# Three feed-forward streams written out with constant waits, their gates spread by DMA instead of by TensorE, and a clamp done by a Relu on ScalarE

## The chip, the cores and the metric

The kernel runs on one NeuronCore of a Trainium2 chip. The metric is device time in microseconds, taken as the median of repeated runs of the whole program. Before the change it is 1961.65 us (three runs, 1959.19 to 1965.57). The engines are named as in the profile: PE is TensorE, PEld its weight loads, DVE is VectorE, ACT ScalarE, POOL GpSimd, and SP issues most of the DMAs.

## The reference

The program is a model of four layers over 2048 tokens of 128 features. Each layer normalises `x`, computes an attention branch `s` and a feed-forward branch, and adds `s * silu(ffn)`:

```
for each layer:
    xn = layernorm(x)
    s  = attention(xn)
    g  = silu(ffn(xn))
    x  = x + s * g
```

The change touches the feed-forward branches of layers 1, 2 and 3, cut here to the core.

```
# layer 1: ternary weights, 512 hidden units (4 blocks of 128)
h   = relu(x @ Wq1.T + b1)
out = h @ Wq2.T + b2

# layer 2: 16 experts of 64 hidden units, 4 chosen per token, and a shared pair
g, u   = silu(x @ w1_e.T), x @ w3_e.T
routed = einsum('tef,ehf,te->th', g * u, w2_e, combine)      # combine: gate of token t for expert e
out    = routed + shared

# layer 3: 16 experts of 128 hidden units, 4 chosen per token
gate = minimum(x @ Wgate_e + bg, 7.0)
up   = clip(x @ Wup_e + bu, -7.0, 7.0)
act  = (up + 1) * gate * sigmoid(1.702 * gate)
out  = einsum('te,teh->th', scores, act @ down_e + down_bias)
```

All experts are computed for all tokens; the gates of the experts that a token did not choose are zero.

## The kernel before

Activations are kept transposed, features on the 128 partitions and tokens along the free axis (`xnT`, 128 x 2048), and worked on in four chunks of 512 tokens (`CHUNK`, `NCH` = 4). A feed-forward branch is a *stream* of steps. One step takes one block of 128 hidden units for one chunk: one or two "up" products of 128 x 512 into PSUM (`f_a`, `f_b`), the activation and the products with the gate on ScalarE and VectorE (`f_act`, `f_mid`, `f_hid`), and one "down" product that accumulates into `f_y`. After the last block of a chunk, ScalarE applies Silu to `f_y` and writes the layer's gate `gT`. The stages are called f1 (layer 1: 4 blocks per chunk, 16 steps), f2 (layer 2: 8 blocks that each hold two routed experts, and one shared block, 36 steps) and f3 (layer 3: 16 experts, 64 steps).

The class `Stream` (L721 to L853) serves all three. It writes one chunk (f1 and f3) or a chunk's steps inside a hardware loop (`Fori`), with waits on register values. There are two PSUM tiles each of `f_a`, `f_b` and `f_g`, and one `f_y`. PE issues the up products of the next step ahead of the down product of the current one.

A token's gate is one number per expert and token, and it has to stand on all 128 partitions to be multiplied into the hidden units. Before, TensorE does that: the gates are split into three bf16 parts (`split3`, L551), the parts are turned by TensorE (`turn_parts`, L1177) and kept as `r_gateT` (48 x 2048 bf16). In each routed step one bf16 product with a 0/1 matrix (`f_g<-r_gateT,r_r_pick`, L769) adds the three parts up and spreads the gate over the partitions, in PSUM, where VectorE's `f_hid` (L850) reads it.

In f3, VectorE clamps: `f_gated` (L822) adds the bias to `f_a` and takes the minimum with 7, then ScalarE computes Silu with slope 1.702 (`f_act`, L801); VectorE computes `f_linear` (L832) from `f_b`, `f_mid` (L836) and `f_hid` (L850). The down bias enters as a product with f32 gates, `f_y<-r_r_gateT,l_down_bias` (L780), first in each chunk.

The routers (`GroupRouter` for layer 2, `SoftmaxRouter` for layer 3, L1146 to L1336) compute the gates during the attention stage of the same layer (a2a, a3a). Their products on TensorE are jobs that a planner in `causal_attention` sets between the attention's own ones, by costs that each router states (`PE_NS`, `DVE_NS`, `CHAIN_NS`).

Of the kernel before, what the change touches and what calls it, by code (L numbers as in the profile page):

```python
# [718 lines left out]


class Stream:  # L721

    def __init__(self, nc, k, ph, J, func, up, down, gate=None, hidden_bias=None, out_bias=0.0, first=None, clamp=None):
        self.nc, self.k, self.J, self.func, self.up, self.down = nc, k, J, func, up, down
        self.gate = gate or (lambda j: None)
        self.hidden_bias, self.out_bias, self.first, self.clamp = hidden_bias, out_bias, first, clamp
        self.U = 1 if J % 2 == 0 else 2
        self.a = [ph.ps(f"a{i}") for i in range(2)]
        self.b = [ph.ps(f"b{i}") for i in range(2)] if len(up(0)) == 2 else None
        self.g = [ph.ps(f"g{i}") for i in range(2)] if gate else None  # L740
        self.y = ph.ps("y")
        self.hid = ph.sb("hid", [P, 2, CHUNK])
        if self.b:
            self.act, self.mid = ph.sb("act", [P, 2, CHUNK]), ph.sb("mid", [P, 2, CHUNK])
        if clamp:
            self.gated, self.linear = ph.sb("gated", [P, 2, CHUNK]), ph.sb("linear", [P, 2, CHUNK])
            self.gated_ready, self.linear_ready = ph.sem("gated"), ph.sem("linear")
        self.up_done, self.act_ready, self.mid_ready = ph.sem("up_done"), ph.sem("act_ready"), ph.sem("mid_ready")
        self.hid_ready, self.hid_used, self.y_read = ph.sem("hid_ready"), ph.sem("hid_used"), ph.sem("y_read")
        self.per = self.U * J  # L750

    def steps(self):

        return [(u, j, u * self.J + j) for u in range(self.U) for j in range(self.J)]

    def chunk(self, tensor, i, u):
        return tensor[:, bass.ds((i * self.U + u) * CHUNK, CHUNK)]

    def tensor(self, pe):
        nc, J, per = self.nc, self.J, self.per  # L760
        pe.sem_inc(self.hid_used, 2)
        with pe.Fori(0, NCH // self.U) as i:
            def up(u, j, n):
                pe.wait_ge(self.hid_ready, i * per + n + 1)
                x = self.chunk(self.k.xnT, i, u)
                for bank, weight in zip((self.a, self.b), self.up(j)):
                    mm = nc.tensor.matmul(bank[n % 2][:], weight, x, start=True, stop=True)
# [2 lines left out]
                mm.then_inc(self.up_done, 1)  # L770

            steps = self.steps()
            up(*steps[0])
            for (u, j, n), after in zip(steps, steps[1:] + [None]):
                if after:
                    up(*after)
                if j == 0:
                    pe.wait_ge(self.y_read, i * self.U + u + 1)
                    if self.first:
                        nc.tensor.matmul(self.y[:], self.first[0], self.chunk(self.first[1], i, u), start=True, stop=False)  # L780
                pe.wait_ge(self.hid_ready, i * per + n + 3)
                nc.tensor.matmul(self.y[:], self.down(j), self.hid[:, n % 2, :], start=(j == 0 and not self.first),
                                 stop=(j == J - 1)).then_inc(self.hid_used, 1)

    def scalar(self, act, between=None):

        act.sem_inc(self.y_read, 1)
        if not self.b:
            act.sem_inc(self.hid_ready, 2)
        if between:  # L790
            self.scalar_chunks(act, 0, 1)
            between()
        self.scalar_chunks(act, 1 if between else 0, NCH // self.U)

    def scalar_chunks(self, act, begin, end):
        nc, J, per = self.nc, self.J, self.per
        with act.Fori(begin, end) as i:
            for u, j, n in self.steps():
                if self.clamp:
                    act.wait_ge(self.gated_ready, i * per + n + 1)  # L800
                    nc.scalar.activation(self.act[:, n % 2, :], self.gated[:, n % 2, :], self.func,  # L801
                                         scale=self.clamp["slope"]).then_inc(self.act_ready, 1)
                elif self.b:
                    act.wait_ge(self.up_done, i * per + n + 1)
                    nc.scalar.activation(self.act[:, n % 2, :], self.a[n % 2][:], self.func).then_inc(self.act_ready, 1)
                else:
                    act.wait_ge(self.up_done, i * per + n + 1)
                    act.wait_ge(self.hid_used, i * per + n + 1)
                    nc.scalar.activation(self.hid[:, n % 2, :], self.a[n % 2][:], self.func,
                                         bias=self.hidden_bias[:, j:j + 1]).then_inc(self.hid_ready, 1)  # L810
                if j == J - 1:
                    act.wait_ge(self.hid_used, i * per + n + 3)
                    nc.scalar.activation(self.chunk(self.k.gT, i, u), self.y[:], ACT.Silu,
                                         bias=self.out_bias).then_inc(self.y_read, 1)

    def vector(self, dve):
        nc, per = self.nc, self.per
        dve.sem_inc(self.hid_ready, 2)
        with dve.Fori(0, NCH // self.U) as i:
            def gated(n, j):  # L820
                dve.wait_ge(self.up_done, i * per + n + 1)
                nc.vector.tensor_scalar(self.gated[:, n % 2, :], self.a[n % 2][:], self.clamp["gate_bias"][:, j:j + 1],  # L822
                                        self.clamp["limit"], ALU.add, ALU.min).then_inc(self.gated_ready, 1)

            for u, j, n in self.steps():
                cur = n % 2
                if self.clamp:
                    gated(n, j)


                    limit = self.clamp["limit"]
                    nc.vector.tensor_scalar(self.linear[:, cur, :], self.b[cur][:], self.clamp["up_bias"][:, j:j + 1],  # L832
                                            limit + 1.0, ALU.add, ALU.min).then_inc(self.linear_ready, 1)
                    dve.wait_ge(self.linear_ready, i * per + n + 1)
                    dve.wait_ge(self.act_ready, i * per + n + 1)
                    nc.vector.scalar_tensor_tensor(out=self.mid[:, cur, :], in0=self.linear[:, cur, :], scalar=1.0 - limit,  # L836
                                                   in1=self.act[:, cur, :], op0=ALU.max, op1=ALU.mult).then_inc(self.mid_ready, 1)
                else:
                    dve.wait_ge(self.act_ready, i * per + n + 1)
                    if self.gate(j) is None:  # L840
                        dve.wait_ge(self.hid_used, i * per + n + 1)
                    out = self.hid if self.gate(j) is None else self.mid
                    mm = nc.vector.tensor_tensor(out[:, cur, :], self.b[cur][:], self.act[:, cur, :], ALU.mult)
                    mm.then_inc(self.mid_ready, 1)
                dve.wait_ge(self.mid_ready, i * per + n + 1)
                if self.gate(j) is None:
                    dve.sem_inc(self.hid_ready, 1)
                else:
                    dve.wait_ge(self.hid_used, i * per + n + 1)
                    nc.vector.scalar_tensor_tensor(out=self.hid[:, cur, :], in0=self.mid[:, cur, :],  # L850
                                                   scalar=1.0 / self.clamp["slope"] if self.clamp else 1.0, in1=self.g[cur][:],
                                                   op0=ALU.mult, op1=ALU.mult).then_inc(self.hid_ready, 1)
# [2323 lines left out]
```

## Time and profile before

| | us |
|---|---|
| Median of three runs | 1961.65 |
| Profiled execution, first to last instruction | 1961.1 |
| TensorE busy | 1627.6 (83%) |
| VectorE busy | 1264.4 (64%) |
| ScalarE busy | 890.3 (45%) |
| f1: first matmul to end of last gate activation | 44.09 |
| f2: the same | 113.50 |
| f3: the same | 216.01 |

The program is a sequence of stages with barriers between them, so that a stage's time is that of its own slowest chain. The three streams are 373.6 us of the span; the rest is attention and layer 0. The granted TensorE clock, averaged over the span, is 0.886 of full speed. In the row of the page that gives it by slice its forty digits run from 5 to 9 tenths (9 stands for 0.9 or more).

### The profile page before, as it was taken

How to read it: one execution, taken by the hardware profiler on the slowest of the kernel's cores; microseconds unless marked ns; L12 is line 12 of the kernel's file. 1: busy time of each engine (PE TensorE's matmuls, PEld its weight loads, DVE VectorE, ACT ScalarE, POOL GpSimd, SP SyncE). 2: the span in 40 equal slices, each digit the busy share in tenths (PEclk: the TensorE clock that was granted, in tenths of full speed). 3: DMA queues.
4: the chain of work that ended last, by engine and by line, in shares of the span. 5: the costliest groups of instructions: out<-in, count | busy, mean ns of one | idle time of the engine just before them, and what ended most of it. 6: DMA issues, size and time to landing. Idle time of an engine off the chain costs nothing. (4 is left out here: it accounts for less than half of the span.)

```text
span 1961.1 us, 33261 instructions
## 1 busy us (share of the span) xinstructions
PE 1627.6 (83%) x12241; PEld 758.7 (39%) x12241; DVE 1264.4 (64%) x2588; ACT 890.3 (45%) x1711; POOL 481.8 (25%) x417
## 2 busy tenths in 40 slices
PE   6989737988888888887579888899659889899998
PEld 4665413433333333343224334333323434343333
DVE  4334768586586676734678888244668887358887
ACT  2332234666565665664236665422316666432221
POOL 1603266565566566410300000000200100000000
PEclk7998856989998998997779999699759999599999
DMA  7232277566575576501421100000340100000000
GB/s 208 89 81 73 62 202 196 154 171 158 148 185 150 149 183 156 132 1 27 138 45 35 34 19 2 1 1 0 90 129 18 35 19 19 1 0 1 0 0 21
DMA packets 211407, 153.63 MB, mean 78 GB/s; under 512 B 57600, under 2 KB 192184, under 8 KB 211128
## 3 DMA queue, kind: packets, MB, share of 16 engines
q1 hardware_dynamic: 201000, 134.90, 26.5%
q10 hardware_dynamic: 8208, 12.52, 2.2%
q0 software_dynamic: 2048, 4.20, 0.7%
q8 instruction: 94, 1.54, 0.3%
q14 instruction: 57, 0.47, 0.1%
HBM read 83.48 MB, written 67.37 MB: 77 GB/s over the span
## 5 line engine op out<-in xcount | busy, mean ns | idle before, releaser
L1936 DVE TENSOR_REDUCE a1a_partial<-a1a_room 128x4 f32<-128x1024 f32 x192 | 225.7, 1220 | 28.3 <-PE a1a_room L2001 27.7
L2376 ACT ACTIVATE a3a_probsT<-a3a_st 128x512 f32<-128x512 f32 (+2 forms) x320 | 155.7, 560 | 131.0 <-PE a3a_st L2442 79.2
L1895 ACT ACTIVATE a1a_probsT<-a1a_st 128x512 f32<-128x512 f32 (+1 forms) x416 | 205.1, 574 | 18.3 <-PE a1a_st L2034 17.5
L2376 ACT ACTIVATE a2a_probsT<-a2a_st 128x512 f32<-128x512 f32 (+2 forms) x320 | 155.6, 560 | 125.3 <-PE a2a_st L2442 73.3
L2288 DVE TENSOR_REDUCE a3a_maxima<-a3a_room 128x2 f32<-128x1024 f32 (+3 forms) x160 | 170.2, 1112 | 38.7 <-PE a3a_room L2411 24.8
L2288 DVE TENSOR_REDUCE a2a_maxima<-a2a_room 128x2 f32<-128x1024 f32 (+3 forms) x160 | 170.2, 1112 | 28.8 <-PE a2a_room L2411 19.1
L2071 PE MATMUL a1a_ctx<-a1a_probsT,a1a_vpad 128*9 128x512 f32 (+3 forms) x1408 | 148.4, 520 | 1.5
L1800 POOL TENSOR_TENSOR a1a_shifted<-a1a_shifted,a1a_best 128x1024 f32<-128x1024 f32 x64 | 121.8, 1903 | 101.8 <-DVE a1a_best L1942 101.7
L1932 DVE CUSTOM_DVE_ANT_0 a1a_shifted<-a1a_room,a1a_bands 128x256 f32<-128x256 f32 x256 | 93.3, 421 | 81.9 <-PE a1a_room L2001 77.1
L2001 PE MATMUL a1a_room<-stack 48*128 48x128 bf16 (+1 forms) x1376 | 110.9, 271 | 40.4 <-DVE a1a_partial L1936 20.7
L1898 ACT ACTIVATE a1a_probsT<-a1a_st 128x512 f32<-128x512 f32 x128 | 73.8, 602 | 129.7 <-PE a1a_st L2043 129.5
L2034 PE MATMUL a1a_st<-stack 51*128 51x512 bf16 (+3 forms) x576 | 113.2, 322 | 14.3 <-ACT a1a_nearT L1902 5.6
L801 ACT ACTIVATE f_act<-f_gated 128x512 f32<-128x512 f32 x64 | 40.3, 629 | 155.6 <-DVE f_gated L822 155.6
L2337 POOL COPY a_vpad<-a_values 128x256 f32<-128x256 f32 x16 | 6.3, 402 | 425.5 <-PE a3a_ctx L2454 209.8
L2435 PE MATMUL a3a_st<-stack 51*128 51x512 bf16 (+3 forms) x384 | 88.9, 357 | 18.5 <-DMA stack<-a3a_parts 9.5
L2435 PE MATMUL a2a_st<-stack 51*128 51x512 bf16 (+3 forms) x384 | 88.1, 354 | 15.5 <-ACT a2a_probsT L2376 8.0
L2454 PE MATMUL a3a_ctx<-a3a_probsT,a_vpad 128*32 128x512 f32 (+3 forms) x768 | 91.0, 552 | 7.7 <-ACT a3a_probsT L2376 4.7
L2001 PEld LDWEIGHTS a1a_room<-stack 48*128 48x128 bf16 x1376 | 47.7, 102 | 126.0 <-DVE a1a_partial L1936 57.8
L2454 PE MATMUL a2a_ctx<-a2a_probsT,a_vpad 128*32 128x512 f32 (+3 forms) x768 | 90.6, 550 | 4.2 <-ACT a2a_ctxT L2383 2.0
L1812 POOL TENSOR_TENSOR a1a_beyond<-a1a_probsT,c_beyond_mask 128x512 f32<-128x512 f32 x56 | 71.1, 1271 | 84.4 <-ACT a1a_probsT L1898 84.4
L2404 PE MATMUL a3a_room<-stack 48*128 48x512 bf16 (+3 forms) x384 | 68.5, 358 | 23.9 <-DMA stack<-k 14.1
L2404 PE MATMUL a2a_room<-stack 48*128 48x512 bf16 (+3 forms) x384 | 66.9, 350 | 25.5 <-PEq L2524 15.9
(500 smaller groups left out, 3276.6 us busy)
## 6 DMA issues: line engine op xcount, KB each, us to landing
a1a_bands<-a_band SPq DMA_DIRECT2D x112, 192.0 KB, 3.9
a_near<-a1a_shifted SPq DMA_DIRECT2D x112, 192.0 KB, 2.9
a1a_near<-a_near SPq DMA_DIRECT2D x64, 256.0 KB, 3.8
a_band<-a1a_r_mix SPq DMA_DIRECT2D x64, 254.0 KB, 3.5
stack<-q SPq DMA_DIRECT2D x96, 96.0 KB
stack<-k SPq DMA_DIRECT2D x32, 96.0 KB
l_inputs<-l_zeros SPq DMA_DIRECT2D x1, 2624.0 KB, 11.1
q<-a1j_parts ACTq DMA_DIRECT2D x10, 256.0 KB, 3.0
```

The source lines that it names most:

```text
L1800: nc.gpsimd.tensor_tensor(shifted[:, V % 2, t], shifted[:, V % 2, t], best[:, V % 2, :, t:t + 1].broadcast_to([P, HG, NEAR]), ALU.subtract ...
L1895: nc.scalar.activation(dst, src, ACT.Exp).then_inc(exp_done, 1)
L1932: ins = nc.vector.tensor_tensor_reduce(shifted[:, V % 2, t, place, :], src[:, place // 2, place % 2, :], band[i][:, place, :], 1.0, LOWEST ...
L1936: nc.vector.tensor_reduce(partial[:, g % 2, :, 1 + r].rearrange("p (a s) -> p a s", a=2), src, X_AXIS, ALU.max).then_inc(job_free, 1)
L2001: mm = nc.tensor.matmul(dst[:, lo + i * P:lo + (i + count) * P], q, rows_of(sides[edge], place, STACK)[:, c * P:(c + count) * P], start=Tr ...
L2034: mm = nc.tensor.matmul(dst[:, to:to + count * P], rows_of(sides[edge], place + j, ALL_ROWS)[:, c * P:(c + 1) * P], query_rows(q_stack, pl ...
L2071: mm = nc.tensor.matmul(ctx[32 * h:32 * h + DH + 1, lo * P:hi * P], vpad[b][right][:, c, h, :], probsT[:, block_index(V, at) % BLOCK_ROOMS ...
L2288: nc.vector.tensor_reduce(best, scores, X_AXIS, ALU.max).then_inc(job_free, 1)
L2376: nc.scalar.activation(probsT[:, block_at % BLOCK_ROOMS, place:place + heads, lo:], src, ACT.Exp).then_inc(exp_done, 1)
L2404: mm = nc.tensor.matmul(dst[:, end - width:end], query_rows(q_stack, place, STACK, I // HALF_TILES)[:, I % HALF_TILES * P:(I % HALF_TILES ...
L2435: mm = nc.tensor.matmul(dst[:, j * width:(j + 1) * width], rows_of(k_stack, place + j, ALL_ROWS)[:, c * P:(c + 1) * P], query_rows(q_stack ...
L2454: mm = nc.tensor.matmul(ctx[32 * PAIRED[h]:32 * PAIRED[h] + 32, lo:], vpad[b][:, c, PAIRED[h], :], probsT[:, block_at % BLOCK_ROOMS, h, lo ...
```

## The change

`Stream`, `run_stream`, `split3`, `turn_parts` and `split_gates` go, and each of the three streams is written out by hand.

- The steps are unrolled, and every wait is on a constant. `f_a` and `f_b` have three PSUM tiles each and `f_y` has two in f2 and f3; f1 has three `f_a` and one `f_y`. PE is two steps ahead with the up products (`AHEAD`). The Silu on `f_y` of a chunk is issued after one or two steps of the next chunk.
- The gates stay f32. They are turned once (`turn_gates`), kept as `r_gateT` (16 x 2048) and stored to DRAM (`store`, by SP, at the end of the attention block). During the stream SP loads them back, spread over 128 partitions, one 128 x 512 f32 tile (256 KB) for each routed step, into four tiles (`GateRows`, `KEPT`). The load for step m waits until the row of step m-4 has been used. VectorE waits for the landing ahead of `f_hid`. The product `f_g` is gone.
- In f3 the clamp moves to ScalarE: `below` = Relu(7 - gate - bias), then Silu(1.702 x 7 - 1.702 x below). VectorE keeps `f_linear`, `f_mid` and `f_hid`.
- The routers have fewer jobs (layer 3: three in place of five) and other costs for the planner. One constant, its load and GpSimd's two `pick` matrices go.

The diff, cut to its core (waits on tiles that are free again and the router's bookkeeping left out):

```diff
-def split3(nc, chain, src, parts, rest):
...
-class Stream:
...
-                if self.gate(j) is not None:
-                    mm = nc.tensor.matmul(self.g[n % 2][:], self.gate(j), self.chunk(self.k.gateT, i, u), start=True, stop=True)
...
+    def store(self, sp, job_free, count):
+        sp.wait_ge(job_free, count)
+        sp.dma_start(self.dram, self.gateT[:]).then_inc(self.stored, 16)
+        sp.wait_ge(self.stored, 16)
+
+class GateRows:
+    KEPT = 4
+    def load(self, sp, m, src, hid_ready, read_by):
+        if m >= self.KEPT:
+            sp.wait_ge(hid_ready, read_by)
+        sp.dma_start(self.of(m), src).then_inc(self.landed[m % self.KEPT], 16)
+    def wait(self, dve, m):
+        dve.wait_ge(self.landed[m % self.KEPT], 16 * (m // self.KEPT + 1))
...
 def grouped_ffn(nc, k, w, tiles, r):
+                for m in range(NCH * M):
+                    c, j = divmod(m, M)
+                    c0, j0 = divmod(m - rows.KEPT, M)
+                    src = over(r.dram[2 * j:2 * j + 2, c * CHUNK:(c + 1) * CHUNK], 1, P // 2)
+                    rows.load(sp, m, src, hid_ready, c0 * J + j0 + 1)
...
+                    rows.wait(dve, c * M + j)
+                    if n >= 3:
+                        dve.wait_ge(hid_used, n - 2)
+                    nc.vector.tensor_tensor(hid[:, n % 3, :], mid[:, n % 2, :], rows.of(c * M + j), ALU.mult).then_inc(hid_ready, 1)
...
 def clamped_ffn(nc, k, w, tiles, r):
+                for n in range(N):
+                    c, j = divmod(n, E)
+                    src = r.dram[j:j + 1, c * CHUNK:(c + 1) * CHUNK].broadcast_to([P, CHUNK])
+                    rows.load(sp, n, src, hid_ready, n - rows.KEPT + 1)
...
+                    nc.scalar.activation(below[:, n % 2, :], a[n % 3][:], ACT.Relu, bias=r.gate_room[:, j:j + 1], scale=-1.0).then_inc(below_ready, 1)
...
+                room_below(0)
+                for n in range(N):
+                    c, j = divmod(n, E)
+                    if n + 1 < N:
+                        room_below(n + 1)
+                    act.wait_ge(below_ready, n + 1)
+                    nc.scalar.activation(acted[:, n % 3, :], below[:, n % 2, :], ACT.Silu, bias=r.top[:, 0:1], scale=-SLOPE).then_inc(act_ready, 1)
+                    if c and j == AHEAD:
+                        gates_of(c - 1)
...
+                router.store(sp, job_free, jobs.index(("router", 0, router.JOBS - 1)) + 1)
```

`over(x, 1, 64)` repeats each row of `x` 64 times, so the source in f2 is 2 rows x 64 repeats x 512 numbers; in f3 it is one row repeated 128 times.

TensorE in f3, before: the first rows of the stage, and the loop that follows (`r_r_each` are the up weights, `l_w_down` the down weights).

```order
L767 MATMUL f_a<-xnT,r_r_each 128x512
L767 MATMUL f_b<-xnT,r_r_each 128x512
L769 MATMUL f_g<-r_gateT,r_r_pick 128x512
L778 REGISTER_ALU
L780 REGISTER_ALU
L780 MATMUL f_y<-r_r_gateT,l_down_bias 128x512
L781 REGISTER_ALU
L782 MATMUL f_y<-f_hid,l_w_down 128x512
L767 MATMUL f_a<-xnT,r_r_each 128x512
L767 MATMUL f_b<-xnT,r_r_each 128x512
L769 MATMUL f_g<-r_gateT,r_r_pick 128x512
```

TensorE in f3, of the changed kernel: the start of the stage.

```order
L1373 MATMUL f_a<-xnT,r_r_each 128x512
L1376 MATMUL f_b<-xnT,r_r_each 128x512
L1387 MATMUL f_y<-r_r_gateT,l_down_bias 128x512
L1389 MATMUL f_y<-f_hid,l_w_down 128x512
L1373 MATMUL f_a<-xnT,r_r_each 128x512
L1376 MATMUL f_b<-xnT,r_r_each 128x512
L1389 MATMUL f_y<-f_hid,l_w_down 128x512
```

`f_g` is gone, the register instructions too, and three steps' up products (of which the last is shown) stand ahead of the first `f_y`.

SP of the changed kernel, from the end of layer 2's attention to the next stage, with the shapes that the destination is written in.

```order
L2400 DMA stack<-a2a_parts 3x8x128 x6
L1059 DMA l_gates<-r_r_gateT 16x2048
L2318 UNCONDITIONAL_BRANCH
L1251 UNCONDITIONAL_BRANCH
L1079 DMA f_rows<-l_gates 128x1x512 x32
L1249 UNCONDITIONAL_BRANCH
```

The same of layer 3:

```order
L2400 DMA stack<-a3a_parts 3x8x128 x6
L1059 DMA l_gates<-r_r_gateT 16x2048
L2318 UNCONDITIONAL_BRANCH
L1359 UNCONDITIONAL_BRANCH
L1079 DMA f_rows<-l_gates 128x512 x64
L1357 UNCONDITIONAL_BRANCH
```

SP had no work in f2 and f3 before; now one store closes the attention block and 32 or 64 row loads stand in the stream.

ScalarE in f1, of the changed kernel (`l_b` holds the biases, `f_std` belongs to layer 1's attention output norm):

```order
L960 ACTIVATE f_hid<-f_a,l_b 128x512 x6
L953 ACT_TABLE_LOAD
L953 ACTIVATE gT<-f_y,l_b 128x512
L960 ACTIVATE f_hid<-f_a,l_b 128x512 x4
L953 ACTIVATE gT<-f_y,l_b 128x512
L949 ACT_TABLE_LOAD
L949 ACTIVATE f_std<-f_std 128x16
L960 ACTIVATE f_hid<-f_a,l_b 128x512 x4
L953 ACT_TABLE_LOAD
L953 ACTIVATE gT<-f_y,l_b 128x512
L960 ACTIVATE f_hid<-f_a,l_b 128x512 x2
L953 ACTIVATE gT<-f_y,l_b 128x512
```

Each chunk of the loop before had one load ahead of its Relus and one ahead of its gate.

## Rows read from the trace of the kernel before

**Rows 1.** Busy time by stretch: columns, f1, f2, f3, then 884 to 896

```profile
core 0: us, PE busy (x) PEld busy (x) DVE busy (x) ACT busy (x) POOL busy (x), PEclk, DMA share, GB/s
872.56:916.65 44.09, 34.13 (x64) 13.07 (x64) 18.60 (x60) 24.91 (x30) 0.00 (x0) 0.88 0.00 0
1270.96:1384.46 113.50, 110.16 (x248) 41.10 (x248) 46.85 (x68) 25.91 (x42) 0.00 (x0) 1.00 0.00 0
1735.21:1951.22 216.01, 207.41 (x456) 75.29 (x456) 178.02 (x256) 47.48 (x72) 0.00 (x0) 0.98 0.00 0
884.00:896.00 12.00, 10.29 (x16) 3.96 (x16) 7.81 (x15) 5.16 (x8) 0.00 (x0) 0.72 0.00 0
```

**Rows 2.** In order of time, a step of f3: start us, us, engine, line

```profile
1746.90 1.12 PE L782 MATMUL f_y<-f_hid,l_w_down 128*128 128x512 f32 x2
...
1747.79 0.63 ACT L801 ACTIVATE f_act<-f_gated 128x512 f32<-128x512 f32 x1 [2.46 <-DVE f_gated L822]
...
1748.52 0.69 DVE L836 SCALAR_TENSOR_TENSOR f_mid<-f_linear,f_act 128x512 f32<-128x512 f32 x1
...
1749.25 0.69 DVE L850 SCALAR_TENSOR_TENSOR f_hid<-f_mid,f_g 128x512 f32<-128x512 f32 x1
...
1749.99 1.12 PE L782 MATMUL f_y<-f_hid,l_w_down 128*128 128x512 f32 x2
```

**Rows 3.** In order of time, f2's shared step, first and last of four

```profile
1294.93 1.02 PE L767 MATMUL f_a<-xnT,r_r_turned 128*128 x2
...
1297.51 1.02 PE L767 MATMUL f_a<-xnT,r_r_turned 128*128 x2
```

**Rows 4.** Groups by line: count, busy us, mean ns, idle before

```profile
L832 DVE TENSOR_SCALAR f_linear<-f_b,r_r_up_bias 128x512 f32<-128x512 f32 x64 | 47.4, 740 | 0.0
...
L769 PE MATMUL f_g<-r_gateT,r_r_pick 48*128 x96 | 37.3, 389 | 0.0
```

**Rows 5.** In order of time, a chunk's end in f3

```profile
1787.10 1.12 PE L782 MATMUL f_y<-f_hid,l_w_down 128*128 128x512 f32 x2 [1.97 <-DVE f_hid L850]
...
1788.36 0.60 ACT L813 ACTIVATE gT<-f_y 128x512 f32 x1 [2.83 <-PE f_y L782]
...
1788.97 1.28 ACT L801 ACT_TABLE_LOAD   x1
...
1791.81 0.75 DVE L822 TENSOR_SCALAR f_gated<-f_a,r_r_gate_bias 128x512 f32<-128x512 f32 x1 [4.77 <-PE f_g L769]
```

**Rows 6.** In order of time, a chunk's end in f1

```profile
878.20 0.69 ACT L809 ACTIVATE f_hid<-f_a,l_b 128x512 f32<-128x512 f32 x1 [1.03 <-PE f_a L767]
878.90 1.28 ACT L813 ACT_TABLE_LOAD   x1
...
884.77 2.08 PE L782 MATMUL f_y<-f_hid,f_w2T 128*128 128x512 f32 x2 [2.99 <-ACT f_hid L809]
```

**Rows 7.** DMA issues of the whole run: count, KB each, us to landing

```profile
a1a_near<-a_near SPq DMA_DIRECT2D x64, 256.0 KB, 3.8
```

**Rows 8.** DMA, 1635.5 to 1637.5 in 40 slices: tenths, GB/s, issues

```profile
DMA  0000000000000000000000002210000000000002
GB/s 0 0 0 0 0 0 0 0 0 0 0 0 0 0 0 0 0 0 0 0 0 0 0 5 51 51 16 0 0 0 0 0 0 0 0 0 0 0 5 51
...
stack<-a3a_parts SPq DMA_DIRECT2D x2, 6.0 KB
```

**Rows 9.** Busy time by stretch, columns as rows 1, during wide loads

```profile
1441.00:1446.00 5.00, 0.61 (x2) 0.11 (x2) 2.30 (x3) 0.00 (x0) 0.00 (x0) 0.50 1.06 354
```

**Rows 10.** DMA, 236.5 to 241 in 40 slices: GB/s

```profile
GB/s 0 0 0 0 0 0 0 0 0 0 0 0 0 0 0 0 0 0 0 0 0 0 0 73 146 237 218 109 255 218 328 401 401 437 382 346 382 382 401 346
```

**Rows 11.** In order of time, the routers' turns in a2a and a3a

```profile
1250.22 1.90 PE L1180 MATMUL a2a_room<-c_ident_bf,r_r_parts 128*48 128x128 bf16 x16
...
1704.41 2.97 PE L1307 MATMUL a3a_room<-c_ident,r_r_gates 128*16 128x128 f32 x16
...
1707.63 0.63 PE L1180 MATMUL a3a_room<-c_ident_bf,r_r_parts 128*48 128x128 bf16 x8 [0.25 <-DVE r_r_gateT L1315]
```

More of the change, by code:

```diff
@@ L718, in _ @@
                 features.scalar(act)
-class Stream:
[L733 to L767, printed above, removed]
-                if self.gate(j) is not None:
-                    mm = nc.tensor.matmul(self.g[n % 2][:], self.gate(j), self.chunk(self.k.gateT, i, u), start=True, stop=True)
[L770 to L852, printed above, removed]
@@ L855, in run_stream @@
-def run_stream(nc, stream):
-    with nc.Block() as block:
-        @block.tensor
-        def _(pe):
-            stream.tensor(pe)
-        @block.scalar
-        def _(act):
-            stream.scalar(act)
-        if stream.b:
-            @block.vector
-            def _(dve):
-                stream.vector(dve)
 def expert_weights(nc, ph, w):
@@ L1076, in _ @@
                         nc.scalar.copy(dst, w_turn[i][:])
-        stream = Stream(nc, k, ph, C, ACT.Relu, up=lambda j: [w1T[:, j, :]], down=lambda j: w2T[:, j, :],
-                        hidden_bias=b1, out_bias=b2[:, 0:1])
+        N, AHEAD, NORM_AFTER = NCH * C, 2, 1
+        a, y, hid = [ph.ps(f"a{i}") for i in range(3)], ph.ps("y"), ph.sb("hid", [P, 3, CHUNK])
+        up_done, hid_ready, hid_used, y_read = ph.sem("up_done"), ph.sem("hid_ready"), ph.sem("hid_used"), ph.sem("y_read")
         stats, moments = ph.sb("stats", [P, NT, 6]), ph.sb("moments", [P, NT, 2])
@@ L1086, in _, with up @@
             def _(pe):
-                stream.tensor(pe)
+                def up(n):
+                    c, j = divmod(n, C)
+                    if n >= 3:
+                        pe.wait_ge(hid_ready, n - 2)
+                    nc.tensor.matmul(a[n % 3][:], w1T[:, j, :], k.xnT[:, c * CHUNK:(c + 1) * CHUNK], start=True, stop=True).then_inc(up_done, 1)
+                for n in range(AHEAD):
+                    up(n)
+                for n in range(N):
+                    c, j = divmod(n, C)
+                    if n + AHEAD < N:
+                        up(n + AHEAD)
+                    if j == 0 and c:
+                        pe.wait_ge(y_read, c)
+                    pe.wait_ge(hid_ready, n + 1)
+                    nc.tensor.matmul(y[:], w2T[:, j, :], hid[:, n % 3, :], start=(j == 0), stop=(j == C - 1)).then_inc(hid_used, 1)
             @block.scalar
@@ L1093, in deviation, with gates_of @@
                     nc.scalar.activation(std[:], std[:], ACT.Sqrt).then_inc(std_ready, 1)
-                stream.scalar(act, deviation)
+                def gates_of(c):
+                    act.wait_ge(hid_used, C * (c + 1))
+                    nc.scalar.activation(k.gT[:, c * CHUNK:(c + 1) * CHUNK], y[:], ACT.Silu, bias=b2[:, 0:1]).then_inc(y_read, 1)
+                for n in range(N):
+                    c, j = divmod(n, C)
+                    act.wait_ge(up_done, n + 1)
+                    if n >= 3:
+                        act.wait_ge(hid_used, n - 2)
+                    nc.scalar.activation(hid[:, n % 3, :], a[n % 3][:], ACT.Relu, bias=b1[:, j:j + 1]).then_inc(hid_ready, 1)
+                    if c and j == AHEAD - 1:
+                        gates_of(c - 1)
+                        if c - 1 == NORM_AFTER:
+                            deviation()
+                gates_of(NCH - 1)
             @block.vector
@@ L1155, in __init__ @@
         self.red = ph.sb("r_red", [P, NT])
-        self.parts = ph.sb("r_parts", [P, NT, 3 * self.E], BF16)
-        k.gateT = ph.sb("gateT", [3 * self.E, TOK], BF16)
-        self.read, self.exp_done, self.split = ph.sem("r_read"), ph.sem("r_exp"), ph.sem("r_split")
+        self.gateT = ph.sb("r_gateT", [self.E, TOK])
+        self.dram = nc.dram_tensor(self.ROWS, [self.E, TOK], F32).ap()
+        self.read, self.exp_done, self.gated, self.stored = ph.sem("r_read"), ph.sem("r_exp"), ph.sem("r_gated"), ph.sem("r_stored")
         self.steps, self.n = ph.sem("r_steps"), 0
@@ L1175, in scalar, with turn_gates @@
         self.nc.scalar.activation(score[:], score[:], ACT.Exp).then_inc(self.exp_done, 1)
-    def turn_parts(self, pe, dst, half):
-        pe.wait_ge(self.split, 1)
+    def turn_gates(self, pe, dst, half):
+        pe.wait_ge(self.gated, 1)
         for t in range(NT // 2):
-            mm = self.nc.tensor.matmul(dst[0:3 * self.E, t * P:(t + 1) * P], self.parts[:, half * NT // 2 + t, :], self.k.ident_bf[:], start=True, stop=True)
+            mm = self.nc.tensor.transpose(dst[0:self.E, t * P:(t + 1) * P], self.tile["gates"][:, half * NT // 2 + t, :], self.k.ident[:])
@@ L1181, in turn_parts, with keep_gates @@
         return mm
-    def keep_parts(self, src, half):
-        return self.nc.vector.tensor_copy(self.k.gateT[:, half * TOK // 2:(half + 1) * TOK // 2], src[0:3 * self.E, :])
-    def split_gates(self, chain):
-        split3(self.nc, chain, self.tile["gates"][:], [self.parts[:, :, self.E * i:self.E * (i + 1)] for i in range(3)], self.tile["rest"][:])
-        chain.mark(self.split)
+    def keep_gates(self, src, half):
+        return self.nc.vector.tensor_copy(self.gateT[:, half * TOK // 2:(half + 1) * TOK // 2], src[0:self.E, :])
@@ new lines, in store, with __init__, of @@
+    def store(self, sp, job_free, count):
[4 more added lines that the diff above has]
+    KEPT = 4
+    def __init__(self, nc, ph):
+        self.tile = ph.sb("rows", [P, self.KEPT, CHUNK])
+        self.landed = [ph.sem(f"rows{i}") for i in range(self.KEPT)]
+    def of(self, m):
+        return self.tile[:, m % self.KEPT, :]
+    def load(self, sp, m, src, hid_ready, read_by):
[4 more added lines that the diff above has]
+        dve.wait_ge(self.landed[m % self.KEPT], 16 * (m // self.KEPT + 1))
@@ L1335, in vector @@
             chain(nc.vector.tensor_tensor(gates[:], gates[:], over(self.red[:], 2, E), ALU.mult))
-            self.split_gates(chain)
+            chain.mark(self.gated)
 def grouped_weights(nc, ph, w):
```

196 lines of the change are left out of this document (152 added, 44 removed).

## The prediction

> **What bounds the kernel now.** I first cut the three streams that the change rewrites out of the span and took each engine's busy time in them, then read a steady step and a chunk's end in order of time, and last the DMA transfers that are like the new loads. From its first matmul to the end of its last gate, the layer-1 stream f1 takes 44.1 us, f2 113.5 us and f3 216.0 us [rows 1]: 373.6 us together, 19% of the time. In f2 and f3 TensorE is busy 97% and 96% of the stretch at a granted clock of 1.00 and 0.98, so there only less TensorE work, or fewer breaks, can pay. In f1 it is busy 34.1 of 44.1 us at 0.88, so there it waits.
>
> The steady step of f3 is 3.09 us, from one f_y to the next (1746.90 to 1749.99) [rows 2]. Three f32 products start 0.86 us apart: in f2's shared step, which spreads no gate, four follow each other from 1294.93 to 1297.51 [rows 3]. Three of them make 2.58 us, and the remaining 0.5 us of a step is the bf16 product that spreads the gate, f_g, 96 times at 389 ns plus its change of operands [rows 4]. At a chunk's end f3 breaks: the last f_y waits 1.97 us, the gate activation follows at 1788.36, a table load of 1.28 us behind it, and the next chunk's first f_gated is at 1791.81, with VectorE idle 4.77 us before it [rows 5]. In f1 a table load stands at each chunk's end (1.28 us at 878.90), TensorE then idles 2.99 us in one piece, and the clock between 884 and 896 averages 0.72 [rows 1, 6].
>
> **The change part by part.** Sums are made against the profiled span of 1961.1 us; it lies 0.5 us under the median of 1961.65, to which I add the sum.
>
> *f1.* The 32 products stay: 32 x 0.86 = 27.5 us. Relu needs no load of its own any more (ScalarE's order, shown with the change, has three loads in the stage), and the rolled loop's breaks go. Left is one y bank: at two chunk ends the next chunk's first f_y stands behind a Relu (0.69 [rows 6]), a load of 1.28 and a gate of about 0.7, less the 0.86 and the last product that TensorE still has: about 1.35 us each, 2.7. The last gate with its handover adds 0.95. Together 31.2 us: **-12.9**. VectorE's layer norm runs beside it and has 28 us to do so. If the clock falls in the two breaks, 2 us of this are lost again.
>
> *f3.* f_g goes from the 64 steps. There remain 64 x 3 products and four bias products: 196 x 0.86 = 168.6 us. At the head TensorE waits about 1.0 us, because the first Silu stands behind two Relus and one table load. At the end the last f_y waits for its chain as now (1.97), and is 0.9 longer at the low clock; the gate with its handover is 0.7. Sum 173.2: **-42.8**. What hides the rest has to hold. VectorE per step has f_linear, f_mid, f_hid, 0.74 + 0.69 + 0.69 [rows 2, 4], with gaps 2.2 to 2.3 us, under 2.58. ScalarE has the new Relu and the Silu, for which no row exists: with a per-partition bias from PSUM the f1 Relu took 0.69 us [rows 6], without it f_act 0.63 [rows 2], so 1.3 to 1.4. The long chain runs from the end of an f_a product to the f_y of the same step: handover 0.14, Relu 0.69, Silu 0.66, f_mid and f_hid 1.38, handovers of 0.03 to 0.10 between them [rows 2, 5], together 3.1 to 3.2. TensorE has four products, 3.44 us, in that place (Relu n+1 is queued ahead of Silu n, so only one step of the two ahead counts). The margin is 0.3 us, hence a rival below.
>
> *Row loads of f3.* 64 loads of 256 KB replace the spreading. VectorE waits for each ahead of f_hid, and behind that stand the next f_linear and with it TensorE. The nearest row, 256 KB to 128 partitions, lands 3.8 us after its issue [rows 7]; four slots at 2.58 us give 10.3 us. The issue costs SP about 0.45 us of an otherwise idle queue. Cover holds; I cost it at nothing. Without it each step would be 3.8 us, which is a rival.
>
> *Row loads of f2.* Here the source is written as two DRAM rows, each repeated 64 times, so the outer count of the source is two; in f3 it is 128. The trace has one transfer with a small outer count: a3a_parts, 24 source rows, written as 3 x 8 x 128. While it runs, the DMA share is 0.2 at 51 GB/s, that is three of the sixteen engines [rows 8]; wide transfers fill the share and move 354 GB/s [rows 9], up to 437 in the best slice [rows 10]. So the side with the smaller outer count sets how many engines work, and I expect two for f2's 32 loads. One engine then moves 354/16 = 22.1 to 437/16 = 27.3 GB/s. Half of 262,144 bytes is 131,072, so a load takes 5.9 to 4.8 us; I take 5.2, a little to the fast side, because two streams share the memory with nobody. They queue one behind another: 32 x 5.2 = 166.4 us. Before that stands the fixed part of a load, about 3.1 us (3.8 less the 0.7 that 16 engines need for its bytes), and after the last landing f_hid, the shared step's f_hid, one f_y and the gate, with handovers 3.2 us. f2 becomes 172.7 us instead of 113.5: **+59.2**, with ends at 4.8 and 5.9 us of +46 and +82. Four slots don't help: they hide a delay, not a rate. Everything else in f2 is shorter than 5.2 us per step (TensorE 2.58), and the gain there of f_g, 20 us, is lost under it.
>
> The Trainium skill, "DMA: Bandwidth & Descriptors", section "Why a DMA increments its semaphore by 16 and not by 1", says that a transfer uses the largest number of engines up to 16 that divides the slowest dimension of both sides: two for f2's loads, sixteen for f3's and for the store. The three-engine row of this case agrees with it, and it speaks against this change: by it the sum is the one below, and without it and that row it would be the first rival's.
>
> *Attention tails.* a3a loses its two groups of bf16 turns (0.63 each [rows 11], with about 0.05 around): **-1.35**. In a2a sixteen bf16 turns of 1.90 us become f32 ones; sixteen of these took 2.97 in a3a [rows 11]: **+1.1**. Store (128 KB) and its wait on SP lie before the block's end with nothing behind them but waits; the split into three parts leaves VectorE while TensorE has other work; a constant load and GpSimd's picks go off the path: nothing.
>
> Sum: -12.9 - 42.8 + 59.2 - 1.35 + 1.1 = **+3.2 us**, 1961.65 + 3.2 = 1965 us. A large gain in f1 and f3 meets a loss of nearly the same size in f2.
>
> **Rivals.** *All sixteen engines carry f2's rows.* Then f2 is bound by TensorE, 108 x 0.86 = 92.9 plus 0.9, -19.7 instead of +59.2: about 1886 us. For it speaks that the destination has 128 partitions; against it the three-engine row. *TensorE falls to 1.2 GHz in f2 (the slower side).* Where it waited 2.99 us in f1, the granted clock fell, to 0.72 on average from 884 to 896 [rows 1, 6]; in f2 it would wait 2.6 us in every step. At half clock a step of three products is 5.16 us, and the shared step has no load to wait for, so f2 is 36 x 5.16 + 3 = 189 us, 16 more: 1981. It decides from the point where the clock stays at 0.5 for most of f2; but at 5.16 of 5.2 TensorE would be busy again, and in f1 the clock came back after a stretch of such work (f1 as a whole has 0.88). *The chain in f3 is longer than 3.44 us.* Each 0.1 us beyond adds 0.05 to a step, 3.2 us in all; at 3.9 us it is 15 us: 1980. *f3's loads don't overlap:* 64 x 3.8 = 243 us, 70 us more; against it, wide transfers run back to back at full share. *The spreading was hidden and f3 gains nothing:* excluded, since f_y follows f_g without idle time on TensorE.
>
> **How the numbers follow.** About 0.3%, 5.9 us, can be told from no change. Two engines at 5.0 to 5.4 us a load, the rest as summed: 0.52, with 1958 to 1972 (0.02 faster, 0.37 within, 0.13 slower). Two engines at the fast end: 0.13, 1950 to 1957, faster. Low clock in f2: 0.11, 1970 to 1982. The slow end of the loads or the longer f3 chain: 0.15, 1966 to 1985 (0.03 within, 0.12 slower). Sixteen engines: 0.07, near 1886. f3's loads not overlapping: 0.02, near 2035. This makes faster 0.22, within 0.40, slower 0.38. The range 1950 to 1982 leaves out the sixteen engines, the loads that don't overlap, and some of both edges.
>
> **What would show it.** f2 about 170 us long, its DMA share near 2/16 = 0.12 all through, row loads 15 to 20 us from issue to landing once four are queued, VectorE's f_hid waiting for DMA, and TensorE waiting for f_hid; f3 about 173 us with f_y 2.58 us apart and no f_hid waiting for a DMA; f1 about 31 us with three table loads. I am wrong if f2's share stands much above 0.12, if its rows come faster than 4.8 us apart, or if f3's step is over 2.7 us.

## The result and the profile after

The changed kernel takes 1972.69 us (median of 15 runs, 1959.22 to 1978.59), the kernel before 1964.27 us beside it (15 runs, 1957.57 to 1968.77). The ratio is 1.0039 with a 95% interval of 1.0021 to 1.0057: 7.7 us more. The interval lies above 1, so the kernel got slower; whether by more than the 0.3% that the prediction took as its bar stays open, as the interval starts below it. The forecast was 1965 us, a sum of +3.2 us and a range of 1950 to 1982.

Nearly nothing in the total shows what happened inside. The three streams, each from its first matmul to the end of its last gate activation, with the columns of [rows 1]:

```profile
core 0: us, PE busy (x) PEld busy (x) DVE busy (x) ACT busy (x) POOL busy (x), PEclk, DMA share, GB/s
877.04:908.32 31.28, 28.43 (x64) 11.80 (x64) 19.09 (x60) 17.46 (x24) 0.00 (x0) 1.00 0.00 1
1265.19:1440.86 175.67, 122.59 (x216) 45.21 (x216) 44.14 (x68) 24.81 (x41) 0.00 (x0) 0.86 0.13 48
1787.85:1962.69 174.84, 171.33 (x392) 73.30 (x392) 131.07 (x192) 86.44 (x133) 0.00 (x0) 0.99 0.34 96
```

f1 fell from 44.09 to 31.28 us and f3 from 216.01 to 174.84, and f2 rose from 113.50 to 175.67: -12.8, -41.2 and +62.2 us, +8.2 together. TensorE is busy 98% of f3, but only 70% of f2, where it was busy 97% before, and the DMA share in f2 is 0.13.

What f2 does in order of time, at its start (start us, us, engine, line, operation, and in brackets the idle time ahead of it and what ended it):

```profile
1272.26 0.69 DVE L1317 TENSOR_TENSOR f_hid<-f_mid,f_rows 128x512 f32<-128x512 f32 x1 [4.32 <-DMA f_rows<-l_gates]
...
1273.01 1.12 PE L1280 MATMUL f_y<-f_hid,r_r_turned 128*128 128x512 f32 x2 [2.43 <-DVE f_hid L1317]
...
1277.54 0.69 DVE L1317 TENSOR_TENSOR f_hid<-f_mid,f_rows 128x512 f32<-128x512 f32 x1 [3.98 <-DMA f_rows<-l_gates]
...
1278.29 1.12 PE L1280 MATMUL f_y<-f_hid,r_r_turned 128*128 128x512 f32 x2 [1.17 <-DVE f_hid L1317]
...
1293.34 0.69 DVE L1317 TENSOR_TENSOR f_hid<-f_mid,f_rows 128x512 f32<-128x512 f32 x1 [3.98 <-issue]
```

VectorE's f_hid waits about 4 us in each step for its row, and comes every 5.27 us (the mean over 32; the third one shown is the fifth of the stage); TensorE's f_y follows it by 0.75 us. Before, the pitch was 3.09 us, in f2's routed steps as in f3's [rows 2]. The waits of the stretch (us in total, times, longest):

```profile
DVE f_hid L1317 <- issue: 103.5, 26, 4.0
PEld f_y L1280 <- DVE f_hid L1317: 81.2, 30, 5.0
...
DVE f_hid L1317 <- DMA f_rows<-l_gates: 21.4, 6, 4.3
```

In 26 of the 32 steps the profile puts VectorE's wait down to "issue" and in 6 to the row loads. The trace's semaphore events settle what it is: in each of the 32 steps the last increment of the row's load comes 0.08 to 0.10 us before f_hid starts. The row loads themselves, in a hundred microseconds of f2 (GB/s by slice, and the queue's packets, MB and share of sixteen engines):

```profile
GB/s 51 49 49 51 49 49 51 49 49 51 49 49 51 49 49 51 49 49 51 49 49 51 49 57 50 49 50 50 49 51 49 49 51 49 49 51 49 49 51 49
...
q1 hardware_dynamic: 2466, 4.97, 13.1%
```

13.1% of sixteen engines is 2.1 engines: about two, busy without a break, at 50 GB/s together. This is the shape of [rows 8], one engine narrower. SP, which issues them (ns min, median, max of one issue), and the fifth of the loads, in order of time:

```profile
L1079 SPq DMA_DIRECT2D f_rows<-l_gates x32: 537/5147/6460, 1265.1 to 1415.3; - x32
...
1273.87 5.15 SPq L1079 DMA_DIRECT2D f_rows<-l_gates  x1
```

The median issue took 5.15 us, about one load's time. The fifth load is issued at 1273.87, and the f_hid that waits for it starts at 1293.34, 19.5 us later.

f3, at its start and in two steady steps:

```profile
1791.40 1.28 ACT L1413 ACT_TABLE_LOAD   x1
...
1795.00 1.12 PE L1389 MATMUL f_y<-f_hid,l_w_down 128*128 128x512 f32 x2 [0.71 <-DVE f_hid L1436]
...
1799.59 0.69 ACT L1399 ACTIVATE f_below<-f_a,r_r_gate_room 128x512 f32<-128x512 f32 x1 [1.28 <-PE f_a L1373]
...
1800.18 0.71 ACT L1413 ACTIVATE f_acted<-f_below,r_r_top 128x512 f32<-128x512 f32 x1
1800.25 1.02 PE L1389 MATMUL f_y<-f_hid,l_w_down 128*128 128x512 f32 x2
...
1800.98 0.69 DVE L1430 SCALAR_TENSOR_TENSOR f_mid<-f_linear,f_acted 128x512 f32<-128x512 f32 x1 [0.49 <-DVE f_linear L1425]
...
1801.70 0.69 DVE L1436 SCALAR_TENSOR_TENSOR f_hid<-f_mid,f_rows 128x512 f32<-128x512 f32 x1
...
1802.83 1.02 PE L1389 MATMUL f_y<-f_hid,l_w_down 128*128 128x512 f32 x2
```

f_y comes every 2.57 us, three products at 0.86 us each, where it was 3.09 [rows 2]. The one table load of the stage stands at its head. Its waits:

```profile
ACT f_below L1399 <- PE f_a L1373: 85.6, 63, 3.4
...
PE f_y L1389 <- DVE f_hid L1436: 2.9, 3, 1.2
```

TensorE waits for f_hid 2.9 us in the whole stage, at its head and its end, and no wait for a row load is among the waits of the stage. The waits at the chunk ends of [rows 5] are gone.

f1, its two chunk ends that have a table load, each with the f_y behind it:

```profile
885.75 1.28 ACT L953 ACT_TABLE_LOAD   x1
...
887.79 1.12 PE L943 MATMUL f_y<-f_hid,f_w2T 128*128 128x512 f32 x2 [1.06 <-ACT gT L953]
...
901.00 1.28 ACT L953 ACT_TABLE_LOAD   x1
...
903.04 1.12 PE L943 MATMUL f_y<-f_hid,f_w2T 128*128 128x512 f32 x2 [1.06 <-ACT gT L953]
```

Where TensorE idled 2.99 us before [rows 6], it idles 1.06 us at two chunk ends, and the granted clock stays at 1.00 in the stage, where it was 0.88. Of the 12.8 us gained, 5.7 are TensorE's busy time (34.13 us before, 28.43 now, for the same 64 matmuls), and 7.1 are time in which it idled.

### The profile page after: what moved, and what is told of

Read it like the earlier page. It is cut to its first block and busy times, and to the rows that moved or that the text cites. A ratio compares the mean times of both kernels' runs of the same rounds, so it can differ in the third digit from the quotient of the medians.

```text
span 1972.6 us, 32899 instructions
## 1 busy us (share of the span) xinstructions
PE 1598.1 (81%) x12129; PEld 757.7 (38%) x12129; DVE 1210.1 (61%) x2514; ACT 919.7 (47%) x1765; POOL 478.8 (24%) x416
## 3 DMA queue, kind: packets, MB, share of 16 engines
q0 software_dynamic: 2048, 4.20, 0.7%
## 5 line engine op out<-in xcount | busy, mean ns | idle before, releaser
L1937 ACT ACTIVATE a1a_probsT<-a1a_st 128x512 f32<-128x512 f32 (+1 forms) x416 | 205.2, 575 | 19.5 <-PE a1a_st L2076 19.1
L2330 DVE TENSOR_REDUCE a3a_maxima<-a3a_room 128x2 f32<-128x1024 f32 (+3 forms) x160 | 170.0, 1113 | 38.2 <-PE a3a_room L2454 25.4
L2043 PE MATMUL a1a_room<-stack 48*128 48x128 bf16 (+1 forms) x1376 | 109.6, 267 | 45.0 <-DVE a1a_partial L1978 24.9
L1317 DVE TENSOR_TENSOR f_hid<-f_mid,f_rows 128x512 f32<-128x512 f32 x32 | 22.2, 692 | 124.9 <-issue 103.5
L1280 PE MATMUL f_y<-f_hid,r_r_turned 128*128 128x512 f32 x72 | 48.0, 756 | 52.4 <-DVE f_hid L1317 52.4
```

What stands on the lines that cost most here:

```text
L1937: nc.scalar.activation(dst, src, ACT.Exp).then_inc(exp_done, 1)
L2043: mm = nc.tensor.matmul(dst[:, lo + i * P:lo + (i + count) * P], q, rows_of(sides[edge], place, STACK)[:, c * P:(c + count) * P], start=Tr ...
L2330: nc.vector.tensor_reduce(best, scores, X_AXIS, ALU.max).then_inc(job_free, 1)
```

## Experiments

The forecast rested on one claim that the trace before could show only from a distance, by a transfer of three engines: that f2's loads run on two DMA engines, and that their rate is f2's time. Theory "engines" says that. Rivals: "row", that a DRAM row read 64 times over is slow whoever reads it; "wait", that the loads start too late; and that the two halves of a load in one DMA are the trouble. The last three experiments are on f3.

**e1: sixteen engines for f2.** Each row load becomes two, one for each half of the partitions, whose source is a single row. The edit is cut to its core here, with the helper that issues the pair written out.

```diff
-src = over(r.dram[2 * j:2 * j + 2, c * CHUNK:(c + 1) * CHUNK], 1, P // 2)
-rows.load(sp, m, src, hid_ready, c0 * J + j0 + 1)
+for i in range(2):
+    src = r.dram[2 * j + i:2 * j + i + 1, c * CHUNK:(c + 1) * CHUNK].broadcast_to([P // 2, CHUNK])
+    sp.dma_start(rows.of(m)[i * P // 2:(i + 1) * P // 2], src).then_inc(rows.landed[m % KEPT], 16)
...
-dve.wait_ge(landed[m % KEPT], 16 * (m // KEPT + 1))
+dve.wait_ge(landed[m % KEPT], 32 * (m // KEPT + 1))
```

> The changed kernel, but each row load of f2 is two loads, one for 64 partitions each, whose source is one DRAM row repeated 64 times; the outer count is then 64 on both sides. Theory 'engines' (f2 is set by two DMA engines that carry 262,144 bytes per step at 5.28 us): all sixteen work, a step's rows need about 0.7 us, and f2 falls from 175.7 us to TensorE's 108 x 0.86 = 92.9 and 2 to 5 us at its ends, 95 to 98 us; the whole about 79 us less, near 1893 us. Rival 'row' (a DRAM row read 64 times over is slow, whatever reads it): f2 stays near 175 us. Rival 'wait' (the loads start too late, since a slot comes free only when its row is used): f2 stays near 175 us, as the slots are the same.

Measured: 1888.43 us, 0.9621 of the kernel before (0.9595 to 0.9647). f2 by stretch, and two of its f_y in order of time:

```profile
1261.37:1354.90 93.53, 92.92 (x216) 40.91 (x216) 46.77 (x68) 24.76 (x41) 0.00 (x0) 1.00 0.33 90
...
1300.05 1.02 PE L1290 MATMUL f_y<-f_hid,r_r_turned 128*128 128x512 f32 x2
...
1302.63 1.02 PE L1290 MATMUL f_y<-f_hid,r_r_turned 128*128 128x512 f32 x2
```

f2 is 93.5 us, TensorE busy 99% of it, f_y 2.57 us apart: with sixteen engines the rows cost nothing. The same bytes from the same DRAM rows, each still read 64 times, so "row" falls; the same four slots, so "wait" falls. It is also the faster kernel, by 73 us against the kernel before, and within 3 us of the 1886 us that the prediction gave to the rival with sixteen engines.

**e2: two loads per step, outer count still two.** As e1, with the 64 repeats written as 2 x 32 (`row` stands for e1's source row).

```diff
-src = row.broadcast_to([P // 2, CHUNK])
+src = over(row.broadcast_to([2, CHUNK]), 1, P // 4)
```

> As the one before, two loads per step, but the source's 64 repeats are written as 2 x 32, so the outer count is two again. 'Engines': both loads of a step go to two engines, 5.28 us per step as in the changed kernel, f2 174 to 178 us at a DMA share of 0.13. If what helps is only that a step's rows come in two loads, f2 is near 96 us.

Measured: one time of 1974.66 us beside 1961.64; f2 by stretch, and two f_hid that follow each other:

```profile
1265.20:1441.80 176.60, 124.22 (x216) 45.92 (x216) 44.14 (x68) 24.81 (x41) 0.00 (x0) 0.86 0.13 48
...
1304.80 0.69 DVE L1327 TENSOR_TENSOR f_hid<-f_mid,f_rows 128x512 f32<-128x512 f32 x1 [3.98 <-issue]
...
1310.07 0.69 DVE L1327 TENSOR_TENSOR f_hid<-f_mid,f_rows 128x512 f32<-128x512 f32 x1 [3.98 <-issue]
```

f2 is 176.6 us at a share of 0.13, f_hid 5.27 us apart: as in the changed kernel. So it wasn't the splitting that helped in e1, but the outer count.

**e3: outer count four.** As e2, with the repeats written as 4 x 16.

> The same with repeats written as 4 x 16. 'Engines': four engines at the same pace, 2.64 us for a step's rows; as the shared steps need none, 32 x 2.64 = 84.5 us of loads lie beside TensorE's 92.9, and f2 is 96 to 101 us with a DMA share near 0.23. 'Row': 175 us.

Measured: one time of 1893.56 us; the same rows:

```profile
1262.70:1360.80 98.10, 94.90 (x216) 41.45 (x216) 46.31 (x68) 24.85 (x41) 0.00 (x0) 0.98 0.23 86
...
1301.74 0.69 DVE L1327 TENSOR_TENSOR f_hid<-f_mid,f_rows 128x512 f32<-128x512 f32 x1
...
1304.32 0.69 DVE L1327 TENSOR_TENSOR f_hid<-f_mid,f_rows 128x512 f32<-128x512 f32 x1
```

f2 is 98.1 us at a share of 0.23, f_hid 2.58 us apart: TensorE bounds the steady step, with almost nothing to spare. Two, four and sixteen engines give f2 176, 98 and 93.5 us. The semaphore events of the traces count the same engines: a load has three of them in f2 of the changed kernel, in e2 and in f3 of e5, five here, and sixteen in e1 and in f3 of the changed kernel, that is one for each engine, and one more where there are fewer than sixteen.

**e4: six slots.** The changed kernel with `KEPT = 6`.

> The changed kernel with six row slots in place of four (f2 and f3). 'Engines': a rate isn't helped by more loads in the queue; f2 174 to 177 us, step 5.28 us, f3 174 to 176 us. 'Wait': two more loads under way at a time shorten f2's step by up to a third, to about 3.6 us, f2 near 125 us.

Measured: one time of 1970.32 us; f2 by stretch, and SP's issues in it:

```profile
1262.50:1438.10 175.60, 121.32 (x216) 45.11 (x216) 44.13 (x68) 24.72 (x41) 0.00 (x0) 0.87 0.13 48
...
L1079 SPq DMA_DIRECT2D f_rows<-l_gates x32: 537/5148/7294, 1262.4 to 1411.8; - x32
```

f2 is 175.6 us, unchanged, and SP's median issue 5.15 us, unchanged. Six slots did not put more loads under way, though: by the semaphore events a load's last increment comes 19.4 us (median) after the start of its issue in both traces, and SP starts each issue when the one before it, 5.15 us long, has ended. So the slots aren't what limits f2; what two more loads really under way would do, this run doesn't show, and "wait" falls by e1 and not by it.

**e5: f3 on two engines.** The reverse test, on the stream that gained.

```diff
-src = r.dram[j:j + 1, c * CHUNK:(c + 1) * CHUNK].broadcast_to([P, CHUNK])
+src = over(r.dram[j:j + 1, c * CHUNK:(c + 1) * CHUNK].broadcast_to([2, CHUNK]), 1, P // 2)
```

> The changed kernel, with f3's row loads written so that the 128 repeats of the one source row are 2 x 64; f2 is left as it is. 'Engines': two engines carry them too, 5.28 us per step, f3 3.1 + 64 x 5.28 + 3 = 344 us instead of 174.8, the whole near 2142 us. If f2 is slow because its source has two different rows, f3, whose repeats are all of one row, stays at 175 us.

Measured: one time of 2132.59 us beside 1965.77; f3 by stretch, and two f_hid that follow each other:

```profile
1784.20:2120.80 336.60, 236.94 (x392) 82.57 (x392) 131.01 (x192) 86.34 (x133) 0.00 (x0) 0.83 0.13 50
...
1899.95 0.69 DVE L1436 SCALAR_TENSOR_TENSOR f_hid<-f_mid,f_rows 128x512 f32<-128x512 f32 x1 [3.08 <-DMA f_rows<-l_gates]
...
1905.12 0.69 DVE L1436 SCALAR_TENSOR_TENSOR f_hid<-f_mid,f_rows 128x512 f32<-128x512 f32 x1 [3.09 <-DMA f_rows<-l_gates]
```

f3 is 336.6 us at a share of 0.13, f_hid 5.17 us apart, 7 us less than expected since a load took 5.17 us here and not 5.28. Nothing but the way of writing 128 repeats differs from the changed kernel, and it costs 162 us.

**e6: a longer chain in f3.**

```diff
-nc.scalar.activation(below[:, n % 2, :], a[n % 3][:], ACT.Relu, bias=r.gate_room[:, j:j + 1], scale=-1.0).then_inc(below_ready, 1)
+nc.scalar.activation(raw[:, n % 2, :], a[n % 3][:], ACT.Relu, bias=r.gate_room[:, j:j + 1], scale=-1.0).then_inc(raw_ready, 1)
+act.wait_ge(raw_ready, n + 1)
+nc.scalar.activation(below[:, n % 2, :], raw[:, n % 2, :], ACT.Relu).then_inc(below_ready, 1)
```

> The changed kernel with one more pass of ScalarE in f3's chain between Relu and Silu (a second Relu of the same numbers, from SBUF to SBUF, about 0.6 us, with 0.1 us of waiting). Theory of the chain: from the end of f_a to the f_y of its step it now takes about 3.05 us of the 3.44 us that four products cover; with 0.7 more it is 3.75, and the step (3.75 + 1.72) / 2 = 2.73 instead of 2.57 us, f3 10 us longer, 185 us. Rival: TensorE bounds f3 however long the chain is, f3 stays within 1 us of 174.8 but for the ends, 176 us.

Measured: one time of 1981.4 us; f3 by stretch, and three f_y with the new operation:

```profile
1782.30:1970.10 187.80, 179.53 (x392) 69.72 (x392) 131.00 (x192) 126.86 (x197) 0.00 (x0) 0.99 0.30 90
...
1861.85 1.02 PE L1390 MATMUL f_y<-f_hid,l_w_down 128*128 128x512 f32 x2
1861.91 0.63 ACT L1402 ACTIVATE f_below<-f_raw 128x512 f32<-128x512 f32 x1
...
1864.71 1.13 PE L1390 MATMUL f_y<-f_hid,l_w_down 128*128 128x512 f32 x2
...
1867.39 1.02 PE L1390 MATMUL f_y<-f_hid,l_w_down 128*128 128x512 f32 x2
```

f3 is 187.8 us, 13 more than in the changed kernel, against 10 expected: f_y alternates between 2.86 and 2.68 us apart, a mean of 2.77. The chain is a bound just behind TensorE, as the margin of 0.3 us had it; a chain 0.7 us longer is seen, though ScalarE itself has room (busy 126.9 of 187.8 us). The edit also frees f_a later, with the second Relu: 27 weight loads of f_a wait for it, 0.2 us at most, beside 56 of f_y that wait for f_hid, up to 2.7 us. So the chain is the larger part, but the two aren't told apart.

**e7: the clamp back on VectorE.** One part of the change undone: `below` is made by VectorE from f_a, ScalarE does only the Silu (cut: `gate_room` then holds the bias itself, and the Silu takes `below` with slope 1.702).

```diff
-nc.scalar.activation(below[:, n % 2, :], a[n % 3][:], ACT.Relu, bias=r.gate_room[:, j:j + 1], scale=-1.0).then_inc(below_ready, 1)
+nc.vector.tensor_scalar(below[:, n % 2, :], a[n % 3][:], r.gate_room[:, j:j + 1], LIMIT, ALU.add, ALU.min).then_inc(below_ready, 1)
```

> The changed kernel with one part undone: f3's clamp is on VectorE again (the bias added and the minimum taken from PSUM, as before the change), ScalarE does the Silu alone. VectorE then has four operations a step, 0.75 + 0.74 + 0.69 + 0.69 = 2.87 us, more than TensorE's 2.57; with gaps 2.9 to 3.0 us a step. f3 is 64 x 2.95 + 8 = 197 us, 18 to 24 us longer than 174.8. Rival, that unrolling and three tiles do all and the clamp's place is free: 175 us.

Measured: one time of 1977.86 us; f3 by stretch, and two f_y, with f_hid and the next f_below between them:

```profile
1780.00:1965.80 185.80, 181.72 (x392) 70.13 (x392) 173.24 (x256) 43.60 (x69) 0.00 (x0) 0.99 0.31 91
...
1861.13 1.13 PE L1389 MATMUL f_y<-f_hid,l_w_down 128*128 128x512 f32 x2
...
1863.22 0.69 DVE L1430 SCALAR_TENSOR_TENSOR f_hid<-f_mid,f_rows 128x512 f32<-128x512 f32 x1
1863.83 0.74 DVE L1415 TENSOR_SCALAR f_below<-f_a,r_r_gate_room 128x512 f32<-128x512 f32 x1
...
1863.96 1.12 PE L1389 MATMUL f_y<-f_hid,l_w_down 128*128 128x512 f32 x2
```

f3 is 185.8 us, 11 more, less than the 18 to 24 expected. The step is 2.83 us after the first few of each chunk, which is VectorE's four operations back to back (VectorE is busy 173.2 of the 185.8 us); I had put gaps between them that aren't there, since f_hid and the next f_below follow at 0.61 us, less than f_hid's own 0.69. So 11 of the 41 us that f3 gained hang on the clamp's place; the other 30 are left for the product that is gone, the unrolling with its third tiles and the chunk ends, which were not tried apart.

## Why the prediction was right, point by point

The mechanism and the sign of each large term held, and the total came out within the range. It is 8 us over the forecast, of which 2.6 are the kernel before (1964.27 us in 15 runs, 1961.65 in the three that the forecast started from); the change itself is +7.7 us where +3.2 was forecast. At 0.39% that falls in the case "slower", to which the prediction had given 0.38, almost as much as to the "within 0.3%" in which its own number lay. In the two profiles the streams and tails together make +7.0 us; by terms the forecast missed 3.0 in f2, 1.6 in f3 and 0.1 in f1, and -0.9 in the tails.

- **f2, +59.2 forecast, +62.2 measured.** Two engines, by the outer count, as the three-engine row [rows 8] had suggested, and e1, e2, e3 and e5 show. By its terms: the load's time was 5.2, and is 5.27 us (1277.54 less 1272.26 is 5.28, and over all 32 it is 5.27), 2.3 us more in all; the fixed part ahead was put at 3.1 us, and the first f_hid starts 7.1 us after the stage's first issue, so it is 1.8; the end after the last landing was put at 3.2 and is 5.2, because the last two f_y ran at half clock (3.78 us for both, granted clock 0.50). The bounds on a load, 4.8 and 5.9 us, held.
- **The rule of the Trainium skill** ("DMA: Bandwidth & Descriptors", "Why a DMA increments its semaphore by 16 and not by 1") named two engines for f2 and sixteen for f3. Shares of 0.13 in f2 and in e5, of 0.23 in e3 where it names four, and of 0.33 at 90 GB/s in e1, where it names sixteen and TensorE is the bound, agree with it; so do the counts of semaphore events under e3.
- **f1, -12.9 forecast, -12.8 measured.** Both table waits are there, 1.06 us long and not 1.35, with the third table load beside other work. That is 0.6 us less than summed, and smaller terms that the sum left out make it up, so that the total agrees to 0.1 us is in part luck.
- **f3, -42.8 forecast, -41.2 measured.** The step is 2.57 us. At the head and the end I had 1.0 and 2.9 us; the head wait is 0.7, and the end 3.0, as the last two f_y wait one after the other (1.18 and 0.99 us) and the last one takes 1.82 us for 1.02. What the sum put at nothing is the start of a chunk: from f_b through the bias product and f_y to the next f_a three products start 0.95, 1.05 and 0.96 us apart (1835.44 to 1838.41 at the second chunk) and not 0.86, 0.4 us more, 1.5 us in four chunks. That is the 1.6 us that f3 lies above its sum. The cover that hides the row loads held: the 64 loads land 3.2 us (median) after their issue, where I took 3.8, and each at least 3.3 us before its f_hid. So did the chain's margin: in the second steady step above f_hid ends at 1802.39 and its f_y starts 0.44 us later, when TensorE comes to it.
- **The rival with the clock fallen** had a part of its mechanism: the granted clock in f2 was 0.86 on average, after 1.00 before, with stretches at half clock inside many steps. But TensorE at half clock stayed inside the 5.27 us, as the forecast argued; only the last two f_y paid, some 2 us. Two steps that follow each other, and the end (columns of [rows 1]):

```profile
1278.30:1283.50 5.20, 2.83 (x6) 1.04 (x6) 1.23 (x3) 0.60 (x1) 0.00 (x0) 1.00 0.13 50
1283.50:1288.80 5.30, 4.39 (x6) 1.35 (x6) 1.33 (x3) 0.60 (x1) 0.00 (x0) 0.68 0.13 49
1436.40:1440.30 3.90, 3.78 (x4) 1.17 (x4) 0.59 (x1) 0.04 (x1) 0.00 (x0) 0.50 0.00 0
```

  The same six matmuls take 2.83 us in one step and 4.39 in the next, and f_hid still comes every 5.27 us.
- **Attention tails, +1.1 and -1.35 forecast.** Mis-sized both. From the end of f1 to the start of f2 it is 356.9 us instead of 354.3, +2.6; from the end of f2 to the start of f3 347.0 instead of 350.8, -3.8. In the first the turns are part of it, sixteen f32 products at a granted clock of 0.50 from 1245.3 to 1249.0, 3.58 us where the bf16 ones took 1.90, also at 0.50, and where I had 2.97 from a3a at a clock of 0.64 [rows 11]; 1.7 us in place of 1.1:

```profile
1245.31 3.58 PE L1050 MATMUL a2a_room<-c_ident,r_r_gates 128*16 128x128 f32 x16
```

  The rest of both I can't name. The seven experiments show the same two numbers within 2 us, so on the side of the change it isn't chance; the kernel before has one trace. I didn't test it.
- **The profiled pair** is 11.5 us apart, of which 4.5 lie ahead of f1, in code that the change hardly touches; f1 starts at 877.0 us there and at 867 to 875 us in the experiments, 872.6 before. I take that part as spread of runs, which the interval of the ratio already has.
- **"Row loads 15 to 20 us from issue to landing"** held as a sign to look for. By the semaphore events the first three loads of f2 land 7.0, 11.7 and 16.4 us after the start of their issue and all others 19.1 to 20.3 us after it, as in the fifth load above. The 3.2 us that the page of the profile gives for `f_rows<-l_gates`, over all 96 loads, is the figure of f3's 64; for a window of f2 alone the view gives none.

## What to carry to other kernels

For a DMA that repeats a few rows over many partitions, look at the outermost count of both sides as they are written, and not at the bytes or the number of partitions: 2 x 64 and 128 move the same numbers, and here one took 5.2 us a tile and the other was hidden under 2.57 us. When a change gains in two places and the total doesn't move, cut the span by stage before judging it; here 54 us of gain lay under 62 us of loss, and one rewritten source took the loss away (0.9621 of the time before). A stream with a chain of four operations across two engines can be close to its bound even two steps ahead: here 0.7 us more in the chain cost 13 us in 64 steps. And a figure for a group of transfers is worth splitting by stage: here one source line issues loads that land after 3.2 us in one stage and after 19.4 us in another.
